# Weight products of a one-core transformer layer as split f16 products, with the keys product and the x loads moved ahead

## What is computed

```python
x = x + xattn(ctx, ctx, layernorm(x), Wk, Wv, bv, Wq, bq, Wo, bo)
#   kp = ctx Wk^T; vp = ctx Wv^T + bv; qp = layernorm(x) Wq^T + bq
#   softmax(qp kp^T / sqrt(512)) vp Wo^T + bo
n = layernorm(x); e = argmax(softmax(n Wg + bg))
x = x + gelu(n W1[e] + b1[e]) W2[e] + b2[e]
```

## Time and profile before

| | us |
|---|---|
| median of 3 runs | 450.68 |
| lowest and highest run | 445.44, 455.07 |
| the profiled execution, own time | 450.37 |
| its span | 448.6 |
| granted TensorE clock, mean | 0.975 |

### The profile page before, as it was taken

The page is one execution under the profiler, slowest core; times in us unless marked ns, Lnnn a source line. Parts: engine busy times, 40 slices in busy tenths (PEclk is TensorE's granted clock), DMA queues, the critical chain, the costliest instruction groups (busy, mean ns, idle before and its releaser), DMA issues.

```text
span 448.6 us, 8708 instructions
## 1 busy us (share of the span) xinstructions
PE 407.2 (91%) x2035; PEld 222.9 (50%) x2035; DVE 323.3 (72%) x655; ACT 248.5 (55%) x568; POOL 241.1 (54%) x305
## 2 busy tenths in 40 slices
PE   6989999798999997987988699999999999899980
PEld 2466664465777675664433244444444444344430
DVE  0276458889467887878988778788878877878750
ACT  1251122857888896865664565555576555555630
POOL 4005923800135787586788255767666675657730
PEclk9988999999999999998899899999999999999997
DMA  8999589960835558436698497798879879698610
GB/s 260 232 391 399 186 290 383 397 220 0 308 96 161 182 175 312 155 127 204 162 306 252 135 272 227 230 257 235 261 226 260 261 225 257 195 275 260 194 56 0
DMA packets 77966, 101.18 MB, mean 226 GB/s; under 512 B 9058, under 2 KB 49006, under 8 KB 76135
## 3 DMA queue, kind: packets, MB, share of 16 engines
q1 hardware_dynamic: 69646, 80.74, 58.6%
q0 software_dynamic: 6400, 19.65, 12.4%
q10 hardware_dynamic: 1880, 0.31, 0.4%
HBM read 70.80 MB, written 31.28 MB: 228 GB/s over the span
## 4 chain that ended last, share of the span: by engine, by line
PE 45%; DVE 16%; DMA 13%; issue 8%; SPq 7%; ACT 6%; POOL 2%; ACTq 1%; DVEq 0%; POOLq 0%
PE bank L1539 14%; PE bank L1542 7%; DMA work<-hidden_blocks 6%; PE bank L1381 4%; PE bank L1490 4%; PE bank L1474 4%; PE bank L1326 4%; SPq L541 3%; DVE expert_weights L1012 3%; DMA expert_weights<-in_x 2%; DVE expert_weights L1156 2%; DVE key_bias_then_xn L1151 2%; PE bank L1466 2%; ACT expert_weights L774 2%; DMA expert_weights<-in_L_ffn_W 2%
## 5 line engine op out<-in xcount | busy, mean ns | idle before, releaser
L1539 PE MATMUL bank<-expert_weights 128*128 x312 | 74.6, 382 | 5.1 <-DVE expert_weights L1156 3.0
L727 POOL DMA_INDIRECT out_x<-keys_values_then_rows_b x39 | 41.0, 1051 | 68.6 <-DVE keys_values_then_rows_b L1239 61.4
L1539 PE MATMUL bank<-expert_weights,ey_bias_split_then_geluT 128*128 x312 | 74.6, 382 | 2.6 <-DVE ey_bias_split_then_geluT L1233 1.6
L909 ACT ACTIVATE work<-work,b_columns 128x128 f32<-128x128 f32 x148 | 47.3, 391 | 22.5 <-DVE work L1228 14.7
L903 ACT ACTIVATE work<-bank 128x512 f32<-128x512 f32 x37 | 22.1, 597 | 57.1 <-PE bank L1542 38.5
L1539 PEld LDWEIGHTS bank<-expert_weights 128*128 128x128 f16 x312 | 30.6, 98 | 44.4 <-issue 11.1
L1228 DVE STREAM_TRANSPOSE work<-work 128x512 f32<-128x512 f32 x37 | 42.5, 1149 | 14.0 <-DMA work<-hidden_blocks 13.7
L1539 PEld LDWEIGHTS bank<-expert_weights,ey_bias_split_then_geluT 128*128 128x128 f16 x312 | 30.7, 98 | 40.5 <-issue 6.5
L774 ACT ACTIVATE expert_weights<-expert_weights 128x512 f16<-128x512 f32 x56 | 33.9, 625 | 26.1 <-DVE expert_weights L1012 22.8
L690 POOL DMA_INDIRECT routed_rows<-work,slot_index x32 | 33.8, 1057 | 25.4 <-DVE slot_index L1101 18.0
L721 POOL TENSOR_TENSOR keys_values_then_rows_b<-keys_values_then_rows_b 128x512 f32<-128x512 f32 x31 | 42.9, 1384 | 7.7 <-POOL keys_values_then_rows_b L713 7.7
(11 more groups left out here) (200 smaller groups left out, 731.0 us busy)
## 6 DMA issues: line engine op xcount, KB each, us to landing
expert_weights<-in_L_ffn_W SPq DMA_DIRECT2D x14, 1024.0 KB, 10.4
...
```

What stands on the lines that cost most here:

```text
L727: pool.indirect_dma_start(out_rows, ids_of, rrow[t.buf][:, 0:D], None, bounds_check=T - 1, oob_is_err=False).then_inc(out_sent[t.buf], 16)
L909: nc.scalar.activation(hid_turned_of(t)[:, P * c:P * (c + 1)], hid_turned_of(t)[:, P * c:P * (c + 1)], ACT.Gelu, bias=b1_cols[:, :, :].rea ...
L1539: mm(o, a[:, c, :], w_split[:, bass.ds(first + (2 * c + h) * D, D)], start=(c == 0 and h == 0 and not begun), stop=False)
```

## The change

KQ, OV and VB become three f16 products each instead of one in f32. ScalarE makes the high parts of Wk and Wq, VectorE the low parts, chunk by chunk, in the memory of expert 1. GpSimd splits Wv in the place of the context as loaded, after the context has been transposed. WOT gets high and low parts (two engines instead of one). The keys are done in front of OV. WVG stands by itself behind VB instead of between the keys, and VGB reads the bias columns broadcast, so the two broadcast copies of VectorE (1022, 1023) go. VG moves from in front of VAL into it, behind the first of the eight, with VectorE's two operations on it (1048, 1052). On the queue of SyncE the context comes ahead of Wo, only expert 0 is loaded between the groups of x, and experts 1 to 3 follow the last group. VectorE's low parts of OV stand behind all moments.

```diff
@@ -236,8 +237,9 @@
 
         kq = work[:, rest:rest + C * D].bitcast(F16).rearrange("p (h c n) -> p h c n", h=2, c=C)
 
-        woT = kvb[:, 0:C, 1, :]
-        bv_bc, bo_cb = (work[:, C * D + D * n:C * D + D * (n + 1)].rearrange("p (c t) -> p c t", c=C) for n in range(2))
+        wk_split, wq_split = (w_of[:, 1, m, :].bitcast(F16).rearrange("p (h c n) -> p h c n", h=2, c=C) for m in range(2))
+        wv_split = work[:, 0:C * D].bitcast(F16).rearrange("p (h c n) -> p h c n", h=2, c=C)
+        woT = kv[:, 0:2 * C * D].bitcast(F16).rearrange("p (c m h n) -> p m h c n", c=C, m=2, h=2)[:, 1]
         val_bias = work[:, C * D + 2 * D:C * D + 3 * D]
 
         bo_bc = kvb[:, B - 2, 1, :]
...
@@ -391,19 +397,19 @@
         J_KQ = job("both", C)
         J_BIAS = job("dve")
         J_GSUM = job("dve")
-        J_WOT = job("act", C)
         J_CTX = job("both", B)
+        J_WOT = job("both", C)
+        J_KEYS = job("act", 2 * C)
         J_OV = job("both", C)
         J_U = job("act")
         J_WOG = job("act")
-        J_KEYS = [job("act") for _ in range(C)]
+        J_VB = job("dve")
         J_WVG = job("act")
-        J_KEYS += [job("act") for _ in range(C)]
-        J_VB = job("dve")
         J_VGB = job("dve")
         J_KB = job("act", 2)
+        J_VAL = [job("dve")]
         J_VG = job("dve")
-        J_VAL = job("dve", B)
+        J_VAL += [job("dve") for _ in range(B - 1)]
...
-            sp.dma_start(wo_sb, chunked(Wo)).then_inc(ld["wo"], 16)
             for h in range(2):
                 sp.dma_start(ctx_nat[0:K, 4 * h:4 * h + 4, :],
                              ctx_in[4 * h:4 * h + 4].rearrange("b k d -> k b d")).then_inc(ctx_half[h], 16)
+            sp.dma_start(wo_sb, chunked(Wo)).then_inc(ld["wo"], 16)
             sp.dma_start(wv_sb, chunked(Wv)).then_inc(ld["wv"], 16)
             for n in range(NM):
                 load_group(n)
+            load_expert(0, w_early[0])
             for n in range(NM, NT // M):
-                if n % NM == 0 and n // NM <= NEARLY - 2:
-                    load_expert(n // NM - 1, w_early[n // NM - 1])
                 load_group(n)
-            load_expert(3, w_early[3])
+            sp.wait_ge(pre_mm, J_KQ + C)
+            for e in range(1, NEARLY - 2):
+                load_expert(e, w_early[e])
 
             sp.wait_ge(stats1, NT)
             load_expert(NEARLY - 2, w_early[NEARLY - 2])
...
+            pool.wait_ge(ld["wv"], 16)
+            pool.wait_ge(pre_mm, J_CTX + B)
+            for e in range(C):
+                link(nc.gpsimd.tensor_scalar(wv_sb[:, e, :], wv_sb[:, e, :], WSCALE, 1.0, ALU.mult, ALU.mult))
+                link(nc.gpsimd.tensor_scalar(wv_split[:, 0, e, :], wv_sb[:, e, :], 1.0, 0.0, ALU.mult, ALU.add))
+                nc.gpsimd.tensor_tensor(wv_split[:, 1, e, :], wv_sb[:, e, :], wv_split[:, 0, e, :], ALU.subtract)\
+                    .then_inc(wv_parts, 1)
             for n in POOL_UNITS:
                 split(n)
...
+            for c in range(C):
+                act.wait_ge(wkq_in[c], 32)
+                for part, w in ((wk_split, wk_sb), (wq_split, wq_sb)):
+                    nc.scalar.activation(part[:, 0, c, :], w[:, c, :], ACT.Copy, scale=WSCALE).then_inc(wkq_high, 1)
             for k in range(C):
                 n = J_KQ + k
-                copy(n, kq[:, 0, k, :], bank[n % 8][:, :], WSCALE)
-            for k in range(C):
-                n = J_WOT + k
-                copy(n, woT[:, k, :], bank[n % 8][:, :])
+                copy(n, kq[:, 0, k, :], bank[n % 8][:, :], 1.0 / WSCALE)
             for b in range(B):
                 n = J_CTX + b
                 copy(n, ctxT[:, 0, :, K * b:K * (b + 1)], bank[n % 8][:, 0:C * K].rearrange("p (c s) -> p c s", c=C))
+            for k in range(C):
+                n = J_WOT + k
+                copy(n, woT[:, 0, k, :], bank[n % 8][:, :], WSCALE)
             act.dma_start(bo_bc, bo.partition_broadcast(P)).then_inc(ld["bo"], 16)
             act.dma_start(bg_bc[:, :], bg.partition_broadcast(P)).then_inc(ld["bg"], 16)
+            for m in range(2 * C):
+                n = J_KEYS + m
+                h, c = m // C, m % C
+                dst = kvb[:, 4 * h:4 * h + 4, 0, P * c:P * c + K]
+                copy(n, dst, bank[n % 8][:, 0:4 * K].rearrange("p (b k) -> p b k", b=4), SCALE / WSCALE)
             for k in range(C):
                 n = J_OV + k
-                copy(n, ov[:, 0, k, :], bank[n % 8][:, :], WSCALE)
-                if k == C - 1:
-                    n = J_U
-                    copy(n, row_weights[:, :, 0], bank[n % 8][:, 0:C], SCALE)
-                    n = J_WOG
-                    copy(n, wo_gate[:, :, :], bank[n % 8][:, 0:C * EM].rearrange("p (c e) -> p c e", c=C))
-            for m in range(2 * C):
-                if m == C:
-                    n = J_WVG
-                    copy(n, row_weights[:, :, 1:1 + EM], bank[n % 8][:, 0:C * EM].rearrange("p (c e) -> p c e", c=C))
-                    act.wait_ge(pre_act, copies("act", J_WVG))
-                    nc.scalar.activation(row_split[:, 0, :, :], row_weights[:, :, :], ACT.Copy, scale=WSCALE)\
-                        .then_inc(rows_split, 1)
-                n = J_KEYS[m]
-                c, h = m // 2, m % 2
-                dst = kvb[:, 4 * h:4 * h + 4, 0, P * c:P * c + K]
-                copy(n, dst, bank[n % 8][:, 0:4 * K].rearrange("p (b k) -> p b k", b=4), SCALE / WSCALE)
-                if m % C == 0:
-                    act.wait_ge(w_early[1 + m // C], 32)
-                for q in range(2):
-                    high(NW + 2 * m + q)
+                copy(n, ov[:, 0, k, :], bank[n % 8][:, :], 1.0 / WSCALE)
+                if k == 1:
+                    act.wait_ge(w_early[1], 32)
+                    for m in range(C):
+                        high(NW + m)
+            n = J_U
+            copy(n, row_weights[:, :, 0], bank[n % 8][:, 0:C], SCALE)
+            n = J_WOG
+            copy(n, wo_gate[:, :, :], bank[n % 8][:, 0:C * EM].rearrange("p (c e) -> p c e", c=C))
+            for m in range(C, NW):
+                high(NW + m)
+            n = J_WVG
+            copy(n, row_weights[:, :, 1:1 + EM], bank[n % 8][:, 0:C * EM].rearrange("p (c e) -> p c e", c=C), 1.0 / WSCALE)
+            act.wait_ge(pre_act, copies("act", J_WVG))
+            nc.scalar.activation(row_split[:, 0, :, :], row_weights[:, :, :], ACT.Copy, scale=WSCALE).then_inc(rows_split, 1)
+            act.wait_ge(w_early[2], 32)
+            for m in range(NW):
+                high(2 * NW + m)
             act.wait_ge(consts, NCONST)
             for h in range(2):
...
+            for c in range(C):
+                for m, (part, w) in enumerate(((wk_split, wk_sb), (wq_split, wq_sb))):
+                    dve.wait_ge(wkq_high, 2 * c + m + 1)
+                    nc.vector.scalar_tensor_tensor(part[:, 1, c, :], w[:, c, :], WSCALE, part[:, 0, c, :], ALU.mult,
+                                                   ALU.subtract).then_inc(wkq_low, 1)
             for k in range(C):
                 n = J_KQ + k
-                low_part(n, [kq[:, h, k, :] for h in range(2)], bank[n % 8][:, :], WSCALE)
+                low_part(n, [kq[:, h, k, :] for h in range(2)], bank[n % 8][:, :], 1.0 / WSCALE)
             n = J_BIAS
             ready(n)
...
+            for k in range(C):
+                n = J_WOT + k
+                low_part(n, [woT[:, h, k, :] for h in range(2)], bank[n % 8][:, :], WSCALE)
...
@@ -1016,49 +1048,53 @@
 
             for n in range(0, NT // M):
                 moments_of_x(n)
-                if n == 3:
-
-                    dve.wait_ge(pre_mm, J_CTX + B)
-                    link(nc.vector.tensor_copy(bv_bc, bcol[:, C:2 * C].unsqueeze(2).to_broadcast([P, C, P])))
-                    link(nc.vector.tensor_copy(bo_cb, bcol[:, 2 * C:3 * C].unsqueeze(2).to_broadcast([P, C, P])))
-                if 3 <= n < 3 + C:
-                    k = n - 3
-                    low_part(J_OV + k, [ov[:, h, k, :] for h in range(2)], bank[(J_OV + k) % 8][:, :], WSCALE)
-            for n in range(NW, 3 * NW):
-                low(n)
-                if n == NW + 9:
-                    dve.wait_ge(rows_split, 1)
-                    nc.vector.scalar_tensor_tensor(row_split[:, 1, :, :], row_weights[:, :, :], WSCALE,
-                                                   row_split[:, 0, :, :], ALU.mult, ALU.subtract)\
-                        .then_inc(rows_split, 1)
-
+
+            def ov_low(k):
+                low_part(J_OV + k, [ov[:, h, k, :] for h in range(2)], bank[(J_OV + k) % 8][:, :], 1.0 / WSCALE)
+
+            ov_low(0)
+            ov_low(1)
+            for m in range(C):
+                low(NW + m)
+            ov_low(2)
+            ov_low(3)
+            for m in range(C, NW):
+                low(NW + m)
+            n = J_VB
+            ready(n)
+            dve.wait_ge(ld["bo"], 16)
```

(54 more changed lines are left out.)

103 lines of the change are left out of this document (49 added, 54 removed).

## The result

| | kernel before | changed kernel |
|---|---|---|
| median | 451.44 us (445.44 to 458.33, 20 runs) | 452.85 us (447.54 to 458.79, 20 runs) |
| span of the profiled execution | 448.6 us | 452.6 us |

The ratio is 1.0077, with a 95% interval of 1.0042 to 1.0111. The change makes the kernel slower by 0.8%, about 3.5 us. The prediction said 443.0, in a range from 436.5 to 450.5, so it missed, and the sign is the other one.

A forecast was written before the change was run, and what follows sets the result against it. Two nearly level preparation chains were taken as the bound: TensorE's products, and VectorE's moments with splits. Loop start 82.9 + 1.45 + 21.3 = 105.6 instead of 113.1; 450.37 - 7.5 = 442.9, about 443 us, range 436.5 to 450.5.

The forecast's parts named there:

- a step of OV: TensorE in the preparation: three f16 products with small U and WOG products, 1.05 us, bounds 0.90 and 1.31.
- the second rival: An OV step stays at 1.31 because small products hide badly: 4.2 us lost, 447 us; chance 0.18.
- GpSimd's split of Wv: Preparation: done at 37.6, hidden by the keys; if not hidden, it would cost up to 10.1 us.
- The moments: VectorE's moments of x in the preparation: done at 59 instead of 74.9, some 16 us earlier.
- TensorE has no wait left from 26.8 on: Preparation from the keys on: TensorE runs without waiting, so the first VAL product is done at 82.9 instead of 91.8.
- is nearly covered: ScalarE's wait for expert 1, due about 60.8, is almost hidden before OV 2 at 62.6; under 3 us.
- the half-level stretch carried over from the kernel before: 3.4 us at half clock, seen in OV before, moves to the keys, which end at 50.0.
- the load's 8.2: Load of expert 1 behind the last group of x: issued at 52.6, there at about 60.8.
- the third rival: The half level takes all of the keys: they cost 16.4 us more, 459 us; chance 0.07.
- VG and the bias row cost 1.45: VectorE's VG and bias row work, now behind the first VAL product, adds 1.45 us before the loop.
- They move as a whole: The two later stages, untouched, shift with the loop's start, 7.5 us earlier, keeping their length within 1 us.
- The late experts: Rival: loads from 52.6 on run slow, expert 5 lands at 112.5, the loop starts late, 456 us; chance 0.05.

The follow-up runs named there:

- e5: The kernel before, unchanged, run again in another batch for a second profile; 450.25 us, ratio 1.0025.
- e6: The changed kernel, unchanged, run again in another batch for a second profile; 452.23 us, ratio 1.0088.
- e1: The changed kernel with ScalarE's OV, U and WOG copies ahead of its wait for expert 1, VectorE's OV low parts likewise together; 445.57 us, ratio 0.9932.
- e3: The changed kernel with 20 f16 products of 512 columns filling TensorE's wait for WOG's copy; 448.34 us, ratio 1.0031.
- e2: e1 with WVG's copy and the row weights' high part after four of expert 1's high parts, not all eight; 446.12 us, ratio 0.9956.
- e7: e2 with 8 of VB's 12 products put between the 16 steps of WVG; 443.72 us over 6 runs.
- e9: e7 with ten f16 products between the last VAL product and the loop, as in e8; 443.17 us over 6 runs.
- e8: e2 with ten f16 products of 512 columns between the last VAL product and the loop; 442.32 us, ratio 0.9871.
- e11: e2 with VG and the bias row ahead of the first VAL product again, on TensorE and VectorE; 446.29 us, ratio 0.9893.
- e12: e8 with 32 f16 products instead of ten ahead of the loop; 445.87 us, ratio 0.9933.
- e13: The kernel before with 32 f16 products put ahead of the loop; 457.13 us, ratio 1.0213.
- e14: The kernel of e8, unchanged, run again in another batch; 444.50 us, ratio 0.9937.

## Why the prediction was wrong

**What held.** The products: 48 of KQ in 12.5 us with their cold start (13.4 predicted), 96 of the keys in 19.6 (19.8), a step of OV 1.01 (1.05), so the second rival, the small products, falls. GpSimd's split of Wv was hidden: it began at 28.4 and OV had no wait. The moments ended at 60.9 (59). From the end of the first VAL product to the loop's 112.41 it took 22.8, predicted 1.45 + 21.3.

**The step that failed** is the one that says of WVG and KB that "TensorE has no wait left from 26.8 on", with its premise that ScalarE's wait for expert 1 "is nearly covered". The mechanism was named, with its price ("if the moments or expert 1 were 5 us later, WVG would wait for WOG's copy"), and it was sized wrong from both sides. TensorE was 5.3 us earlier at the end of OV (61.5, not 66.8): 3.4 of it because the half-level stretch carried over from the kernel before did not come (e5 shows that it isn't a fixed part of the kernel before either), 0.9 from the start of the keys, the rest from OV's steps. Expert 1 landed at 64.8, not 60.8: its load started 2.1 later and took 10.04, not 8.2. Together 9.3 of which 5 were cover; the wait was 4.48. For the load's 8.2 the prediction gives no working. In e6 the load landed at 61.3, close to the forecast, and a wait of 1.98 came all the same, because OV ended 6.3 us early: the products that were priced too high used up the cover by themselves. What made TensorE earlier was worth nothing, because ScalarE's order tied it to a load. I counted the two chances of being off one by one, and not against each other.

**The term that was missing** is the clock behind that wait and behind the tiny products. WVG cost 7.0 instead of 3.8, VGB 3.4 instead of 1.9, KB 7.8 instead of 5.04, 7.4 us together, nearly all of it at the granted 0.50. With the wait it is 11.9 us against a head start of 5.3: the first VAL product 6.7 late (89.6 against 82.9). In e6 the same terms are 1.98 and 6.2 against a head start of 6.3, and the product is 2.0 late. e1 gets 8.5 us back. e3 shows the part of the clock that hangs on the wait, some 3.3 us in WVG; the slow VGB and KB stay in e1, e2 and e3, so they are put down to the run of tiny products, which the change put in one place (e7 and e9 speak for it, with one profile each). The forecast and the third rival had the half level in the wrong place, in the keys behind a gap ahead of 24.9, where the trace shows none. A rule bears on this. The Trainium skill (TensorE: Matmul & The Clock Gate, HAM oscillation — how this bites in real kernels) describes how a wait for a transfer between bursts of products brings the array back to the half clock, so that the next burst starts cold and takes longer. The trace agrees behind the 4.48 us, where WVG took 6.97 instead of 3.67 in e3. Behind the tiny products the clock fell without a wait too (e2, e3).

**The loop's start.** The prediction let VG and the bias row cost 1.45 and that was right. It did not see that the idle time ahead of the loop grows with it, from 1.43 to 2.23, and that the first tiles then run at the low clock: 2.6 us up to tile 4's exp by e6 and e2, 1.4 in the first profile of the changed kernel, gone in e8 and e11. In that profile it shows as 1.09 for the transposes at 112.41 and a first exp at 116.0, 0.6 later than before in spite of 0.7 gained.

**The later stages.** "They move as a whole" was the last step of the sum, and e12 and e13 contradict it in both directions. Between the two profiles shown, 3.4 of the 4.0 us of difference arise between tile 28's exp and the first hidden copy. But e13 and e12 show this passage long without the change and short with it, so it can't be put down to the change. In e6 the loop starts 4.6 us earlier than in the changed kernel's first profile, and only 1.6 are left at the end: 1.2 go to a longer low clock at the loop's start, 3.3 to the low stretch in the loop, and 1.5 come back behind it. By the first exps the kernels with a mended order (e1, e2, e8, e11, e14) start the loop 6 to 12 us earlier than the kernel before, and by the medians they gain 3 to 6. So the wait and the low clock explain that the forecast gain of 7.5 us was lost. They don't explain the 0.8% on top: in e6 the loop starts 3.6 to 5.3 us earlier than in the two profiles of the kernel before, and yet the changed kernel is slower in both batches. That cause stays open.

**The late experts** were no rival to count at first: the loads ran at 397 GB/s from 68 to 86. They became a bound in e7, when all ahead of them was mended.
